# A table written in one contiguous transfer, and the products of a deformable convolution on GpSimd between its gathers

## The chip, the cores and the metric

The kernel runs on one core of one Trainium2 chip. The metric is the device time of the program in microseconds. Three timed runs gave 628.83, 629.05 and 629.80 us; the median is 629.05 us.

## The reference

Four layers follow each other on a batch of four images x of shape (4, 128, 32, 32), float32:

- L0: attention with 32 reduced channels, over the 1024 pixels of an image, with a projection and a residual.
- L1: a bottleneck with a deformable convolution, and a residual. This is where the change lies.
- L2: attention with 16 channels for queries and keys and 128 for values, scaled by gamma, and a residual.
- L3: group norm, attention with 128 channels, projection, residual, divided by the root of 2.

The deformable convolution samples each pixel's nine taps at positions that are themselves computed:

```
off  = conv3x3(h, woff) + boff
y, x = off + base of pixel and tap
mask = sigmoid(off[:, 18:])
samp = (img[y0, x0]*wy0*wx0 + img[y0, x0+1]*wy0*wx1
      + img[y0+1, x0]*wy1*wx0 + img[y0+1, x0+1]*wy1*wx1) * mask
out  = einsum('bckhw,ock->bohw', samp, w2) + b2
```

## The kernel before, in words

Each layer works on one image at a time, with 1024 pixels as eight tiles of 128. The engines' instructions are written out by hand, one program for each engine, with semaphores between them. A first loop of four turns does L0 of image a together with the first part of L1 of image b = a - 1. A second loop does L3 of image a, L2 of image b = a + 1 and the last part of L1, the samples, of image c = a + 2. The last turn of the first loop takes the samples of image 0 in; the first turn of the second loop has no L3, and those of image 1; the last two turns have no samples.

The path of the samples, which the change touches:

- `l1_cells` (ScalarE) writes the 32 channels of the image four times into `cells`, shifted by one row or column, so that one column of `cells` holds the 4 corners x 32 channels of one cell. There are 33 x 33 = 1089 cells.
- `l1_table`: TensorE transposes `cells` in nine chunks of up to 128 columns (the last has 65), ScalarE copies them to `tabS`, and SP writes them to a table in DRAM, `cell_table0` or `cell_table1`, one row of 512 bytes for each cell. Before, this takes two DMAs for an image: 1024 rows in pieces of one row each, and the last 65.
- `l1_coordinates` (VectorE) computes the rows to fetch, `rows_all`, and the weights of the corners, `corner_w`, for the whole image.
- GpSimd (POOL) copies the rows to `rows_cur`, waits for the table (`tab_out`), and then, for each of the eight tiles, waits for a free slot (`slot_free`) and issues nine indirect DMAs (L309), one for each tap: 128 pixels x one row of 512 bytes, into `got[:, t, k, :]`. `got` has eight slots, one for each tile.
- `l1_weigh` (VectorE, L1167) waits until a tile's nine gathers are in (`got_sem[t]`), multiplies 128 x 1152 values by the weights of the corners, each of 36 weights for 32 channels, into `weighed`, and frees the slot. `l1_add` (L1180) adds the four corners into `samples`. Both stand at fixed places in VectorE's order, between the maxima, copies and reciprocals of L2 and L3.
- `l1_turn` (TensorE, ScalarE) transposes the samples into `samplesT`; `l1_conv2` and `l1_conv3` are matmuls over them, and `l1_end` gives the input of L2.

Of the kernel before, what the change touches and what calls it, by code (L numbers as in the profile page):

```python
# [20 lines left out]
N = H * W  # L21
P = 128
# [9 lines left out]
CELLS = H + 1  # L32
TABLE = CELLS * CELLS
TCHUNKS = -(-TABLE // P)
TLAST = TABLE - (TCHUNKS - 1) * P
YX = 2 * TAPS
OFFS = 3 * TAPS
TAPS_A_TURN = 3
# [24 lines left out]
def build(nc, x_dram, weights_dram, out_dram):  # L63
# [5 lines left out]
    with ctx:  # L69
# [4 lines left out]
            return ctx.enter_context(nc.semaphore(name))  # L74


        tables = [nc.dram_tensor(f"cell_table{n}", (TABLE, CORNERS * R), fp32).ap() for n in range(2)]


        wts = sb("wts", [P, WIDTH])  # L80
# [30 lines left out]
        cells = sb("cells", [P, CELLS, CELLS])  # L111
        tabS = sb("tabS", [P, BATCH, TCHUNKS, P])
        x3s = y = cells[:, :, :].rearrange("p a b -> p (a b)")[:, 0:N]


        h2_full = x2_sum = sb("h2_full_x2_sum", [P, N])
# [14 lines left out]
        weighed = sb("weighed", [P, TAPS, CORNERS * R])  # L131
# [79 lines left out]
        sp_go, pool_go = sem("sp_go"), sem("pool_go")  # L211
        got_sem = [sem(f"got{t}") for t in range(TILES)]
        slot_free = sem("slot_free")
        sample_ready = sem("sample_ready")
        st_mm = sem("st_mm")
        st_copied = sem("st_copied")
# [40 lines left out]
        @block.sync  # L257
        def _(sp):
            sp.dma_start(wts[:, 0:FIRST], weights_dram[:, 0:FIRST]).then_inc(weights0_in, 16)
            for b in range(1, BATCH):  # L260
                sp.dma_start(xall[:, b, :], x_view[b]).then_inc(x_in[b], 16)
            tab_pair = tabS[:, :, :, :].rearrange("p (a n) k d -> p a n k d", n=2)
            with sp.Fori(0, BATCH // 2) as i:
                for n, table in enumerate(tables):

                    sp.wait_ge(tab_copied, 6 * i + 3 * n + 3)
                    sp.sem_inc(sp_go, 1)

# [12 lines left out]

            for h in range(2):
                at = slice(h * HALF, (h + 1) * HALF)
                sp.wait_ge(y_ready, BATCH + 1 + h)
                sp.dma_start(out_view[BATCH - 1, :, at], y[:, at]).then_inc(y_out, 16)
            sp.wait_ge(y_out, 16 + 16 * (BATCH + 1))
            for n in range(2):
                sp.wait_ge(tab_out[n], 16 * BATCH)


        @block.gpsimd
        def _(pool):
            rows_pair = rows_all[:, :, :].rearrange("p (a n) k -> p a n k", n=2)
            with pool.Fori(0, BATCH // 2) as i:
                for n, table in enumerate(tables):

                    pool.wait_ge(rows_ready, 2 * i + n + 1)
                    nc.gpsimd.tensor_copy(rows_cur[:, n, :],
                                          rows_pair[:, bass.ds(i, 1), n, :].rearrange("p a k -> p (a k)"))\
                        .then_inc(rows_copied, 1)  # L300
                    pool.wait_ge(rows_copied, 2 * i + n + 1)
                    pool.wait_ge(tab_out[n], 32 * i + 32)
# [12 lines left out]
        def _(pe):  # L315
# [137 lines left out]

            def l1_table(i, n, bank):

                flat = cells[:, :, :].rearrange("p a b -> p (a b)")
# [341 lines left out]
        def _(act):  # L798
# [58 lines left out]
            def l1_table(i, n, bank):  # L857
                act.wait_ge(tab_mm, 3 * i + n + 1)
                first, chunks = PIECES[n][0], len(PIECES[n])
                rows = P if first < TCHUNKS - 1 else TLAST  # L860
                to = tabS[0:rows, bass.ds(i, 1), first:first + chunks, :].rearrange("p i k d -> p (i k) d")
                copy(to, bank[0:rows, 0:chunks * P].rearrange("p (k d) -> p k d", d=P)).then_inc(tab_copied, 1)


            def l1_turn(i, t, bank):
# [211 lines left out]
        def _(dve):  # L1077
# [23 lines left out]

            def l0_denominators(i, samples_too):
                if samples_too:
                    l1_samples(0, 0)
                dve.wait_ge(d4_mm, i + 1)
                nc.vector.tensor_copy(d4, (ys if samples_too else xq)[:, :]).then_inc(d4_copied, 1)
                if samples_too:
                    l1_samples(0, 1)
                    l1_samples(0, 2)
                dve.wait_ge(d_mm, i + 1)  # L1110
                nc.vector.reciprocal(inv[:, :], ys[:, 0:TILES]).then_inc(inv0_done, 1)
                if samples_too:
                    l1_samples(0, 3)

            def l0_end(i):

# [43 lines left out]
                last.then_inc(corner_ready, 1)  # L1160


            def l1_weigh(i, t):

                dve.wait_ge(got_sem[t], 16 * TAPS * (i + 1))
                w = corner_w[:, bass.ds(i, 1), t, :].rearrange("p b k -> p (b k)")
                nc.vector.tensor_tensor(weighed[:, :, :].rearrange("p k (c r) -> p (k c) r", r=R),  # L1167
                                        got[:, t, :, :].rearrange("p k (c r) -> p (k c) r", r=R),
                                        w.rearrange("p (k a) -> p k a", a=1).to_broadcast([P, TAPS * CORNERS, R]),
                                        ALU.mult).then_inc(slot_free, 1)  # L1170
                dve.drain()
                if t == TILES - 1:
                    dve.sem_inc(table_free, 1)

            def l1_add(i, t, early=False):

                if t >= 2 or early:

                    dve.wait_ge(st_mm, TILES * i + t - 1)
                nc.vector.tensor_reduce(samples[:, t % 2, :].rearrange("p (k r) -> p k r", r=R),  # L1180
                                        weighed[:, :, :].rearrange("p k (c r) -> p k r c", r=R),
                                        axis=X, op=ALU.add).then_inc(sample_ready, 1)
                dve.drain()

            def l1_samples(i, t, early=False):
                l1_weigh(i, t)
                l1_add(i, t, early)

            def l1_conv2(i):
                dve.wait_ge(h2_high, 2 * i + 2)  # L1190
# [103 lines left out]
            def second_loop_step(a, b, c):  # L1294
# [15 lines left out]
                for t in range(TILES):  # L1310
                    if L3:
                        l3_turn(a, t)
                    if L2 and t == 0:
                        maximum(2, b, 1, xs)
                    if SAMPLES and t >= 3:
                        l1_weigh(c, t - start)
                    if L3:
                        if t + 1 < TILES:
                            l3_max(a, t + 1, (ys if L2 else (ys, xs)[(t + 1) % 2]))
# [9 lines left out]
                        l2_values(b, 0)  # L1329
                        l2_values(b, 1)  # L1330
                if SAMPLES:
                    l1_samples(c, TILES - start)
                if L3 and L2:
                    l3_end(a)
                elif L3:
# [2 lines left out]
                if L2:  # L1338
                    for n in range(2, TILES):
                        l2_values(b, n)  # L1340
                        if SAMPLES and L3:
                            if n == 2:
                                l1_samples(c, 6)
                            if n == 3:
                                l1_weigh(c, 7)
# [14 lines left out]
                    l2_statistics(1)  # L1360


            nc.vector.memset(cells[:, :, :], 0.0)
# [38 lines left out]
            first_loop_step(BATCH - 1, BATCH - 2, None, samples_too=True)  # L1402

            for t in range(4, TILES):
                l1_samples(0, t)
            for t in range(2):
                l1_samples(1, t, early=True)
            l1_conv2(0)
            l1_end(0)
            l1_coordinates(BATCH - 1, xp)  # L1410
# [88 lines left out]
```

## Time and profile before

| | |
|---|---|
| timed, median of 3 | 629.05 us |
| profiled execution, span | 852.6 us |
| POOL busy | 283.4 us, 33% |
| TensorE busy, matmul | 531.5 us, 62% |
| VectorE busy | 353.6 us, 41% |
| ScalarE busy | 277.5 us, 33% |
| mean granted clock | 0.794 |
| moved by DMA | 27.11 MB, mean 32 GB/s |

The profiled execution's own time is known here only by its span. It is 223.6 us longer than the median of the timed runs, so a duration or an order can be taken from the profile, but a sum of its waits can't be set equal to a sum of the timed run's. Busy shares are averages over stages with different limits. A matmul's end is modelled, and spans of POOL are rough.

### The profile page before, as it was taken

Reading aid. Unit: us, or ns where it says so; the run is one execution under the profiler, and the core shown is the slowest. Engines: PE = TensorE matmul, PEld = TensorE weight load, DVE = VectorE, ACT = ScalarE, POOL = GpSimd, SP = SyncE. Lnnn points to the kernel's source line nnn. Section 1 sums busy time; section 2 is a strip of 40 time slices with the busy share of each in tenths; the row PEclk is TensorE's granted clock in tenths of the full one; section 3 lists DMA queues with packets and bytes.
Section 4 is the critical chain, followed back from the end, with each engine's and each line's share of the span. In section 5 each row is a group of like instructions: output and inputs, shape, how many; then the busy total and the mean of one; then the engine's idle time right before and its main releaser. Section 6 shows DMA issues by size and latency. Waiting matters only on the chain.

```text
span 852.6 us, 7735 instructions
## 1 busy us (share of the span) xinstructions
PE 531.5 (62%) x2840; PEld 362.9 (43%) x2840; DVE 353.6 (41%) x462; ACT 277.5 (33%) x402; POOL 283.4 (33%) x296
## 2 busy tenths in 40 slices
PE   5789930117883065026604897271859998999797
PEld 2445410113542033014502665151636785678576
DVE  4244420002671193129400586151347984752243
ACT  1436510005550041104100554130235633554353
POOL 0000477750037477734775006565520000000000
PEclk8697975558996578556756899585889999999899
DMA  4000111110001121100211001111100000000000
GB/s 166 0 1 1 52 52 53 52 40 26 1 22 53 37 63 52 52 26 22 76 52 43 1 2 40 43 41 43 59 22 0 0 25 0 1 1 16 10 1 25
DMA packets 15298, 27.11 MB, mean 32 GB/s; under 512 B 4900, under 2 KB 9256, under 8 KB 15144
## 3 DMA queue, kind: packets, MB, share of 16 engines
q0 software_dynamic: 9216, 18.89, 7.8%
q1 hardware_dynamic: 5768, 6.20, 2.2%
q10 hardware_dynamic: 288, 1.67, 0.5%
q8 instruction: 17, 0.28, 0.1%
q14 instruction: 9, 0.07, 0.0%
HBM read 22.41 MB, written 4.33 MB: 31 GB/s over the span
## 4 chain that ended last, share of the span: by engine, by line
PE 41%; another core or an unknown queue 30%; DVE 11%; issue 8%; ACT 7%; DVEq 2%; DMA 1%; ACTq 0%
PE ys L559 6%; PE yy L581 5%; PE xq L346 5%; DVE samples L1180 3%; PE yy L572 3%; DVE neg_max L1086 2%; ACT expT L805 2%; PE ys L479 2%; PE xq L319 2%; PE yy L319 2%; PE ys L319 2%; PE xs L325 2%; DVE weighed L1167 2%; PE xq L389 1%
## 5 line engine op out<-in xcount | busy, mean ns | idle before, releaser
L309 POOL DMA_INDIRECT got<-cell_table,rows_cur x288 | 282.2, 980 | 247.5 <-DVE weighed L1167 149.3
L346 PE MATMUL xq<-vT,expT 128*128 128x129 f32 x512 | 68.8, 294 | 14.9 <-ACT oT L898 7.3
L581 PE MATMUL yy<-v3T,probsT 128*128 128x128 f32 x512 | 65.1, 282 | 16.2 <-issue 15.3
L346 PEld LDWEIGHTS xq<-vT,expT 128*128 128x128 f32 x512 | 66.8, 210 | 19.5 <-issue 9.5
L581 PEld LDWEIGHTS yy<-v3T,probsT 128*128 128x128 f32 x512 | 61.7, 196 | 24.5 <-issue 20.2
L1180 DVE TENSOR_REDUCE samples<-weighed 128x288 f32<-128x1152 f32 x32 | 68.9, 2153 | 2.2 <-issue 0.7
L559 PE MATMUL ys<-k,q_offs 128*128 128x512 f32 x112 | 55.1, 616 | 1.3 <-ACT k L924 1.3
L1264 DVE TENSOR_REDUCE neg_max<-ys 128x1 f32<-128x1024 f32 x28 | 34.2, 1222 | 38.6 <-PE ys L559 35.7
L1210 DVE RECIPROCAL inv<-xq 128x1 f32<-128x1 f32 x32 | 5.3, 167 | 103.2 <-remote 68.6
L479 PE MATMUL ys<-samplesT,wts 96*128 96x512 f32 x48 | 29.8, 772 | 27.7 <-issue 27.1
L470 PE MATMUL yy<-wts,samples 128*96 128x128 f32 x72 | 14.1, 313 | 52.2 <-ACT samplesT L800 43.5
L1086 DVE TENSOR_REDUCE neg_max<-xs 128x1 f32<-128x1024 f32 x32 | 38.9, 1217 | 15.1 <-remote 8.6
L1269 DVE COPY probsT<-yy 128x512 f32<-128x512 f32 x32 | 22.0, 689 | 53.9 <-PE yy L572 46.6
L1167 DVE TENSOR_TENSOR weighed<-got,corner_w 128x1152 f32<-128x1152 f32 x32 | 43.5, 1359 | 1.3 <-issue 0.5
L898 ACT ACTIVATE oT<-xq,inv 128x128 f32<-128x128 f32 x28 | 10.3, 367 | 94.9 <-DVE inv L1210 65.2
L572 PE MATMUL yy<-wts,probs 128*128 128x128 f32 x224 | 35.1, 280 | 6.8 <-ACT probs L930 4.8
L800 ACT ACTIVATE samplesT<-yy 96x384 f32<-96x384 f32 x24 | 11.7, 485 | 72.0 <-remote 45.3
L470 PEld LDWEIGHTS yy<-wts,samples 128*96 128x96 f32 x72 | 8.8, 142 | 61.4 <-issue 56.1
L805 ACT ACTIVATE expT<-xs 128x1024 f32<-128x1024 f32 x32 | 32.7, 1020 | 6.2 <-remote 4.3
L572 PEld LDWEIGHTS yy<-wts,probs 128*128 128x128 f32 x224 | 26.3, 143 | 19.1 <-issue 7.6
L930 ACT ACTIVATE probs<-ys,neg_max 128x1024 f32<-128x1024 f32 x28 | 31.2, 1114 | 6.2 <-DVE neg_max L1264 6.1
L340 PE MATMUL ys<-q_stack,k_stack 128*128 128x512 f32 x32 | 14.1, 528 | 30.4 <-issue 19.3
(186 smaller groups left out, 875.4 us busy)
## 6 DMA issues: line engine op xcount, KB each, us to landing
got<-cell_table,rows_cur POOLq DMA_INDIRECT x288
cell_table<-tabS SPq DMA_DIRECT2D x4, 512.0 KB
xall<-x_dram SPq DMA_DIRECT2D x3, 512.0 KB, 9.3
out_dram<-cells SPq DMA_DIRECT2D x3, 512.0 KB, 2.7
wts<-weights_dram ACTq DMA_DIRECT2D x1, 1120.5 KB, 8.9
xall<-x_dram ACTq DMA_DIRECT2D x1, 512.0 KB, 5.0
out_dram<-cells SPq DMA_DIRECT2D x2, 256.0 KB, 2.0
wts<-weights_dram SPq DMA_DIRECT2D x1, 289.0 KB, 4.8
```

Source lines behind the costliest of these rows:

```text
L309: nc.gpsimd.indirect_dma_start(got[:, t, k, :], None, table, bass.IndirectOffsetOnAxis(ap=rows_cur[:, n, at:at + 1], axis=0)).then_inc(got ...
L319: last = nc.tensor.matmul(bank, w, x[:, at], start=True, stop=True)
L346: last = nc.tensor.matmul(to, expT[:, j, t * P:(t + 1) * P], vT[:, j, C - width:C + 1], start=j == 0, stop=j == TILES - 1)
L479: last = nc.tensor.matmul(bank, wt("w2", TR)[:, g * P:(g + 1) * P], samplesT[:, g, at], start=g == 0, stop=g == TURNS - 1)
L559: last = nc.tensor.matmul(to, q3[:, t * P:(t + 1) * P], k3[:, at], start=True, stop=True)
L572: last = nc.tensor.transpose(bank[:, j * P:(j + 1) * P], probs[:, t % 2, at:at + P], ident)
L581: last = nc.tensor.matmul(yo[:, 0:C], probsT[:, j * P:(j + 1) * P], v3T[:, j, :], start=j == 0, stop=j == TILES - 1)
L805: nc.scalar.activation(expT[:, j, :], bank[:, :], ACT.Exp).then_inc(exp_done[L], 1)
L1086: nc.vector.tensor_reduce(neg_max[:, t:t + 1], bank[:, :], axis=X, op=ALU.max, negate=True).then_inc(max_done[L], 1)
L1167: nc.vector.tensor_tensor(weighed[:, :, :].rearrange("p k (c r) -> p (k c) r", r=R), got[:, t, :, :].rearrange("p k (c r) -> p (k c) r", r=R),
L1180: nc.vector.tensor_reduce(samples[:, t % 2, :].rearrange("p (k r) -> p k r", r=R), weighed[:, :, :].rearrange("p k (c r) -> p k r c", r=R) ...
L1264: nc.vector.tensor_reduce(neg_max3[:, t:t + 1], pair[:, :], axis=X, op=ALU.max, negate=True).then_inc(max3_done, 1)
```

## The change

The table in DRAM is padded to 1152 rows. TensorE transposes every ninth column of `cells` (chunk k has the columns 9p + k), so that partition p of `tabS` holds nine rows that lie next to each other in the table, and one DMA for each image writes them, 4608 bytes for each partition. The rows that the gathers fetch are the same.

The multiplication by the corners' weights moves from VectorE to POOL, in place in `got`. POOL issues the gathers of tile t, then multiplies tile t - 1; the last tile's product comes after all gathers of its image. VectorE keeps the addition, which now reads `got`, waits for POOL's `weighed`, and frees the slot afterwards. In VectorE's order the additions stand where products and additions stood, in part later by one step.

```diff
-        tables = [nc.dram_tensor(f"cell_table{n}", (TABLE, CORNERS * R), fp32).ap() for n in range(2)]
+        tables = [nc.dram_tensor(f"cell_table{n}", (PADDED, CORNERS * R), fp32).ap() for n in range(2)]
...
+        cells_padded = sb("cells", [P, PADDED])
+        cells = cells_padded[:, 0:TABLE].rearrange("p (a b) -> p a b", b=CELLS)
...
-                    sp.dma_start(table[0:(TCHUNKS - 1) * P, :].rearrange("(k p) d -> p k d", p=P),
-                                 tab_pair[:, bass.ds(i, 1), n, 0:TCHUNKS - 1, :].rearrange("p a k d -> p (a k) d"))\
-                        .then_inc(tab_out[n], 16)
-                    sp.dma_start(table[(TCHUNKS - 1) * P:TABLE, :],
-                                 tab_pair[0:TLAST, bass.ds(i, 1), n, TCHUNKS - 1, :].rearrange("p a d -> p (a d)"))\
+                    sp.dma_start(table.rearrange("(p k) d -> p (k d)", k=TCHUNKS),
+                                 tab_pair[:, bass.ds(i, 1), n, :, :].rearrange("p a k d -> p (a k d)"))\
                         .then_inc(tab_out[n], 16)
...
+            def weigh(i, n, t):
+                pool.wait_ge(got_sem[t], 16 * TAPS * (2 * i + n + 1))
+                pool.sem_inc(pool_go, 1)
+                parts = got[:, t, :, :].rearrange("p k (c r) -> p (k c) r", r=R)
+                nc.gpsimd.tensor_tensor(parts, parts,
+                                        weight_pair[:, bass.ds(i, 1), n, t, :].rearrange("p a (k b) -> p (a k) b", b=1)
+                                        .to_broadcast([P, TAPS * CORNERS, R]), ALU.mult).then_inc(weighed, 1)
...
                         for k in range(TAPS):
                             at = t * TAPS + k
                             nc.gpsimd.indirect_dma_start(
                                 got[:, t, k, :], None, table,
                                 bass.IndirectOffsetOnAxis(ap=rows_cur[:, n, at:at + 1], axis=0)).then_inc(got_sem[t], 16)
+                        if t == 1:
+                            pool.wait_ge(corner_ready, 2 * i + n + 1)
+                            pool.sem_inc(pool_go, 1)
+                        if t:
+                            weigh(i, n, t - 1)
+                    weigh(i, n, TILES - 1)
...
-                    rows = P if k < TCHUNKS - 1 else TLAST
-                    last = nc.tensor.transpose(bank[0:rows, k % 4 * P:(k % 4 + 1) * P],
-                                               flat[:, k * P:k * P + rows], ident)
+                    last = nc.tensor.transpose(bank[:, k % 4 * P:(k % 4 + 1) * P], strided[:, k, :], ident)
...
-            def l1_weigh(i, t):
-                dve.wait_ge(got_sem[t], 16 * TAPS * (i + 1))
-                w = corner_w[:, bass.ds(i, 1), t, :].rearrange("p b k -> p (b k)")
-                nc.vector.tensor_tensor(weighed[:, :, :].rearrange("p k (c r) -> p (k c) r", r=R),
-                                        got[:, t, :, :].rearrange("p k (c r) -> p (k c) r", r=R),
-                                        w.rearrange("p (k a) -> p k a", a=1).to_broadcast([P, TAPS * CORNERS, R]),
-                                        ALU.mult).then_inc(slot_free, 1)
-                dve.drain()
+            def l1_add(i, t, early=False):
+                dve.wait_ge(weighed, TILES * i + t + 1)
+                if t >= 2 or early:
+                    dve.wait_ge(st_mm, TILES * i + t - 1)
+                nc.vector.tensor_reduce(samples[:, t % 2, :].rearrange("p (k r) -> p k r", r=R),
+                                        got[:, t, :, :].rearrange("p k (c r) -> p k r c", r=R),
+                                        axis=X, op=ALU.add).then_inc(sample_ready, 1)
+                dve.drain()
+                dve.sem_inc(slot_free, 1)
                 if t == TILES - 1:
                     dve.sem_inc(table_free, 1)
```

## Rows read from the trace of the kernel before

**Rows 1.** The page: span, busy time, and POOL's busy tenths in 40 slices.
```profile
span 852.6 us, 7735 instructions
...
PE 531.5 (62%) x2840; PEld 362.9 (43%) x2840; DVE 353.6 (41%) x462; ACT 277.5 (33%) x402; POOL 283.4 (33%) x296
...
POOL 0000477750037477734775006565520000000000
```

**Rows 2.** The page: the chain that ended last, by engine.
```profile
PE 41%; another core or an unknown queue 30%; DVE 11%; issue 8%; ACT 7%; DVEq 2%; DMA 1%; ACTq 0%
```

**Rows 3.** Timelines of TensorE and VectorE: start us, us, engine, line, operation.
```profile
112.70 0.73 PE L325 MATMUL ys<-k_stack,q_stack 96*128 96x512 f32 x2 [0.29 <-issue]
...
140.88 1.22 DVE L1086 TENSOR_REDUCE neg_max<-ys 128x1 f32<-128x1024 f32 x1 [18.39 <-remote]
```

**Rows 4.** Stretches: length, busy us of PE, PEld, DVE, ACT, POOL; clock, DMA share, GB/s.
```profile
94.00:185.00 91.00, 21.77 (x106) 13.59 (x106) 14.99 (x15) 12.29 (x16) 69.08 (x72) 0.63 0.18 51
...
626.00:718.00 92.00, 83.54 (x483) 60.87 (x484) 67.52 (x81) 45.03 (x71) 0.00 (x0) 0.94 0.02 7
```

**Rows 5.** Timeline of POOL: gathers of the first image; duration ns min/median/max of all.
```profile
94.18 1.11 POOL L309 DMA_INDIRECT got<-cell_table,rows_cur  x1 [11.91 <-DMA cell_table<-tabS]
95.59 0.94 POOL L309 DMA_INDIRECT got<-cell_table,rows_cur  x1 [0.30 <-issue]
...
183.96 0.94 POOL L309 DMA_INDIRECT got<-cell_table,rows_cur  x1 [0.30 <-issue]
...
L309 POOL DMA_INDIRECT got<-cell_table,rows_cur x288: 938/944/2128, 94.2 to 624.8; - x144
```

**Rows 6.** The page: groups of gathers, reductions and products, busy us and mean ns.
```profile
L309 POOL DMA_INDIRECT got<-cell_table,rows_cur x288 | 282.2, 980 | 247.5 <-DVE weighed L1167 149.3
...
L1180 DVE TENSOR_REDUCE samples<-weighed 128x288 f32<-128x1152 f32 x32 | 68.9, 2153 | 2.2 <-issue 0.7
...
L1167 DVE TENSOR_TENSOR weighed<-got,corner_w 128x1152 f32<-128x1152 f32 x32 | 43.5, 1359 | 1.3 <-issue 0.5
```

**Rows 7.** Timeline of VectorE and POOL: a product and a gather.
```profile
305.67 1.36 DVE L1167 TENSOR_TENSOR weighed<-got,corner_w 128x1152 f32<-128x1152 f32 x1
305.75 2.10 POOL L309 DMA_INDIRECT got<-cell_table,rows_cur  x1 [0.31 <-issue]
```

**Rows 8.** Timeline of SP, and the page's DMA issues.
```profile
88.52 0.50 SPq L274 DMA_DIRECT2D cell_table<-tabS  x1
...
out_dram<-cells SPq DMA_DIRECT2D x3, 512.0 KB, 2.7
...
out_dram<-cells SPq DMA_DIRECT2D x2, 256.0 KB, 2.0
```

**Rows 9.** Timeline of VectorE: the end of two turns, and the last product.
```profile
629.20 0.74 DVE L1222 SCALAR_TENSOR_TENSOR x<-xs,wts,xall 128x512 f32<-128x512 f32 x1
...
703.44 1.36 DVE L1167 TENSOR_TENSOR weighed<-got,corner_w 128x1152 f32<-128x1152 f32 x1
...
718.62 0.74 DVE L1222 SCALAR_TENSOR_TENSOR x<-xs,wts,xall 128x512 f32<-128x512 f32 x1
```

**Rows 10.** Waits: engine, line, waited for, us in total, times, longest.
```profile
POOL got L309 <- DVE weighed L1167: 149.3, 6, 51.1
```

**Rows 11.** Groups of POOL by shape: copy and smallest fill.
```profile
L298 POOL COPY rows_cur<-rows_all 128x72 int32 x4 | 1.0, 246 | 94.6 <-DVE rows_all L1141 94.6
...
L1491 POOL MEMSET const-float32-0.0<- 128x1 f32 x1 | 0.1, 98 | 0.3 <-issue 0.3
```

**Rows 12.** Timeline of VectorE: low parts of three turns, first product.
```profile
57.96 1.22 DVE L1081 SCALAR_TENSOR_TENSOR k_stack<-yy,k_stack 32x1024 fp32r<-32x1024 f32 x1 [0.49 <-ACT k_stack L800]
...
102.34 1.22 DVE L1081 SCALAR_TENSOR_TENSOR k_stack<-yy,k_stack 32x1024 fp32r<-32x1024 f32 x1 [0.49 <-ACT k_stack L800]
...
219.94 1.22 DVE L1081 SCALAR_TENSOR_TENSOR k_stack<-yy,k_stack 32x1024 fp32r<-32x1024 f32 x1 [0.49 <-ACT k_stack L800]
...
243.15 1.35 DVE L1167 TENSOR_TENSOR weighed<-got,corner_w 128x1152 f32<-128x1152 f32 x1
```

More of the change, by code:

```diff
@@ L34 @@
 TCHUNKS = -(-TABLE // P)
-TLAST = TABLE - (TCHUNKS - 1) * P
+PADDED = TCHUNKS * P
 YX = 2 * TAPS
@@ L110, in build @@
         bn_t = sb("bn_t", [P, 3])
-        cells = sb("cells", [P, CELLS, CELLS])
+        cells_padded = sb("cells", [P, PADDED])
+        cells = cells_padded[:, 0:TABLE].rearrange("p (a b) -> p a b", b=CELLS)
         tabS = sb("tabS", [P, BATCH, TCHUNKS, P])
-        x3s = y = cells[:, :, :].rearrange("p a b -> p (a b)")[:, 0:N]
+        x3s = y = cells_padded[:, 0:N]
         h2_full = x2_sum = sb("h2_full_x2_sum", [P, N])
@@ L130, in build @@
         got = sb("got", [P, TILES, TAPS, CORNERS * R])
-        weighed = sb("weighed", [P, TAPS, CORNERS * R])
         samples = sb("samples", [P, 2, TAPS * R])
@@ L213, in build @@
         slot_free = sem("slot_free")
+        weighed = sem("weighed")
         sample_ready = sem("sample_ready")
@@ L287, in _ @@
             for n in range(2):
-                sp.wait_ge(tab_out[n], 16 * BATCH)
+                sp.wait_ge(tab_out[n], 16 * (BATCH // 2))
         @block.gpsimd
@@ L293, in _ @@
             rows_pair = rows_all[:, :, :].rearrange("p (a n) k -> p a n k", n=2)
+            weight_pair = corner_w[:, :, :, :].rearrange("p (a n) t k -> p a n t k", n=2)
+            def weigh(i, n, t):
[5 more added lines that the diff above has]
+                                        .to_broadcast([P, TAPS * CORNERS, R]), ALU.mult).then_inc(weighed, 1)
             with pool.Fori(0, BATCH // 2) as i:
@@ L301, in _ @@
                     pool.wait_ge(rows_copied, 2 * i + n + 1)
-                    pool.wait_ge(tab_out[n], 32 * i + 32)
+                    pool.wait_ge(tab_out[n], 16 * i + 16)
                     for t in range(TILES):
@@ L454, in l1_table @@
             def l1_table(i, n, bank):
-                flat = cells[:, :, :].rearrange("p a b -> p (a b)")
+                strided = cells_padded[:, :].rearrange("p (a k) -> p k a", k=TCHUNKS)
                 for k in PIECES[n]:
-                    rows = P if k < TCHUNKS - 1 else TLAST
-                    last = nc.tensor.transpose(bank[0:rows, k % 4 * P:(k % 4 + 1) * P],
-                                               flat[:, k * P:k * P + rows], ident)
+                    last = nc.tensor.transpose(bank[:, k % 4 * P:(k % 4 + 1) * P], strided[:, k, :], ident)
                 last.then_inc(tab_mm, 1)
@@ L859, in l1_table @@
                 first, chunks = PIECES[n][0], len(PIECES[n])
-                rows = P if first < TCHUNKS - 1 else TLAST
-                to = tabS[0:rows, bass.ds(i, 1), first:first + chunks, :].rearrange("p i k d -> p (i k) d")
-                copy(to, bank[0:rows, 0:chunks * P].rearrange("p (k d) -> p k d", d=P)).then_inc(tab_copied, 1)
+                to = tabS[:, bass.ds(i, 1), first:first + chunks, :].rearrange("p i k d -> p (i k) d")
+                copy(to, bank[:, 0:chunks * P].rearrange("p (k d) -> p k d", d=P)).then_inc(tab_copied, 1)
             def l1_turn(i, t, bank):
@@ L1103, in l0_denominators @@
                 if samples_too:
-                    l1_samples(0, 0)
+                    l1_add(0, 0)
                 dve.wait_ge(d4_mm, i + 1)
@@ L1107, in l0_denominators @@
                 if samples_too:
-                    l1_samples(0, 1)
-                    l1_samples(0, 2)
+                    l1_add(0, 1)
+                    l1_add(0, 2)
                 dve.wait_ge(d_mm, i + 1)
@@ L1112, in l0_denominators @@
                 if samples_too:
-                    l1_samples(0, 3)
+                    l1_add(0, 3)
             def l0_end(i):
@@ L1180, in l1_add @@
                 nc.vector.tensor_reduce(samples[:, t % 2, :].rearrange("p (k r) -> p k r", r=R),
-                                        weighed[:, :, :].rearrange("p k (c r) -> p k r c", r=R),
+                                        got[:, t, :, :].rearrange("p k (c r) -> p k r c", r=R),
                                         axis=X, op=ALU.add).then_inc(sample_ready, 1)
                 dve.drain()
-            def l1_samples(i, t, early=False):
-                l1_weigh(i, t)
-                l1_add(i, t, early)
+                dve.sem_inc(slot_free, 1)
+                if t == TILES - 1:
+                    dve.sem_inc(table_free, 1)
             def l1_conv2(i):
@@ L1314, in second_loop_step @@
                         maximum(2, b, 1, xs)
-                    if SAMPLES and t >= 3:
-                        l1_weigh(c, t - start)
                     if L3:
@@ L1331, in second_loop_step @@
                 if SAMPLES:
-                    l1_samples(c, TILES - start)
+                    l1_add(c, TILES - start)
                 if L3 and L2:
@@ L1342, in second_loop_step @@
                             if n == 2:
-                                l1_samples(c, 6)
-                            if n == 3:
-                                l1_weigh(c, 7)
+                                l1_add(c, 6)
                             if n == 4:
@@ L1360, in second_loop_step @@
                     l2_statistics(1)
-            nc.vector.memset(cells[:, :, :], 0.0)
+            nc.vector.memset(cells_padded[:, :], 0.0)
             nc.vector.memset(shift[:, :, :], 0.0)
@@ L1404, in _ @@
             for t in range(4, TILES):
-                l1_samples(0, t)
+                l1_add(0, t)
             for t in range(2):
-                l1_samples(1, t, early=True)
+                l1_add(1, t, early=True)
             l1_conv2(0)
```

2 lines of the change are left out of this document (removed).

## The prediction

> **What bounds the kernel now.** The profiled execution spans 852.6 us, while the three timed runs have a median of 629.05 us: 223.6 us apart, so the first task is to find out which parts of the profile the timed runs don't have. The busy shares come first [rows 1]: no engine is full, and GpSimd (POOL) works in blocks that end near three quarters of the span. The chain that ended last [rows 2] gives 30% of the span, about 256 us, to "another core or an unknown queue", though the program has one core. Two rows show what this is [rows 3]: VectorE waits 18.39 us and reads only at 140.88 scores whose matmuls TensorE shows at 112.70. The stretches [rows 4] say when it happens. From 94 to 185 us POOL issues all 72 gathers of one image, and TensorE is busy for 21.8 of 91 us at a granted clock of 0.63. After 626 us no gather is left, TensorE is busy for 83.5 of 92 us, and the granted clock is 0.94. So the unexplained waits go with the gathers, and their sum is near what the timed runs lack. I take them for a cost of the recorded execution, and rebuild the timed one from two lines that these waits don't touch. That is a choice; the trace doesn't prove it.
>
> **The gather line.** Nine gathers fetch one tile, eight tiles make an image, and there are four images: 288 gathers. The first starts at 94.18 us, the 72nd at 183.96, and the median instruction is 0.944 us with 0.30 us between two [rows 5], 1.248 from start to start (of the 71 steps from the first gather to the last, 89.78 us, or 1.265 each with the lengthened ones). An image takes 72 x 1.248 = 89.9 us. The sum of all 288 [rows 6] is 282.2 us, 10.3 more than 288 x 0.944 = 271.9. Gathers that are lengthened explain that excess: one took 2.10 us beside a product that VectorE ran from 305.67 us [rows 7]. Landing after issue isn't shown for a gather; the nearest rows are output transfers, 2.0 us for 256 KB [rows 8]. Back to back, the last tile is there at 94.2 + 4 x 89.9 + 10.3 + 2.0 = 466.1 us. In the profile, the last product starts at 703.44 us and the span ends 149.2 us later, all of it without gathers [rows 9]. Together: 615.3 us.
>
> **The engine line.** In the same undisturbed part the start of one turn of the second loop can be read from VectorE's last additions of the turn before, 629.20 and 718.62 us [rows 9]: 89.4 us a turn, against 89.9 for an image's gathers. The two are level, so gathers that grow longer can't hide. The waits of POOL for VectorE, 149.3 us in six places [rows 10], don't speak against this: they are the engines' delays of the recorded execution, handed on through buffers that come free late.
>
> Against the median, 629.05 - 615.3 = 13.8 us remain: what lies around the span, and what my line leaves out. I carry them unchanged.
>
> **The change, part by part.**
>
> *Table in one DMA.* Before, the second of the first table's two DMAs is issued at 88.52 us, and the gather that waits for both starts at 94.18 [rows 5, 8]: 5.7 us. Output of the same 512 KB with long rows lands in 2.7 us [rows 8]; with 4.6 KB runs I expect about that, so the gathers start 3 us earlier, at 91.2. The bounds are no gain and 5.7 us. Later tables are written while POOL still gathers the image before, and that cover is kept, as POOL becomes later. The strided transposes and the last chunk's 128 rows instead of 65 cost TensorE and ScalarE at most some tenths of a microsecond for each table, beside the image's attention; without that cover, only the first table's would count.
>
> *The product moves to POOL.* VectorE loses 32 products of 1.36 us, 43.5 us in all [rows 6]. Its reduction (2.15 us) keeps its size. POOL gains 32 products, and queues behind each are the next tile's nine gathers; SP's queue is not passed. Price of one: the trace has no such operation on POOL. The lower bound is VectorE's 1.36 us for the same shape. For POOL itself, a fill of one element takes 0.10 us and a copy of 72 elements 0.246 [rows 11]: 0.1 us fixed and 2.0 ns an element, so 1152 elements cost 0.1 + 2.3 = 2.4 us with one source. A product reads two sources; at twice that it is 4.7 us, the upper bound. I take 2.4, since the second source here is only one value for every 32 elements, and with the issue gap of 0.3 it is 2.7 us.
>
> The Trainium skill (GPSIMD Engine Reference, Elementwise — side-by-side cycle accounting) gives 4497 ns as measured for a tensor_tensor add of 2048 elements on GpSimd, 1.96 times VectorE's; scaled to 1152 that is an estimate of 2.53 us, which would add 4 us to my sum. Its table of engine selection advises against elementwise work there.
>
> *New waits.* Product t-1 comes after gathers t, so 11.2 us cover the landing. The eighth product has no gathers in front of it and waits for its tile: 2.0 us an image, and behind it stand the next image's gathers. An image on POOL then costs 89.9 + 8 x 2.7 + 2.0 = 113.5 us. The wait for the weights of the corners at tile 1 costs nothing: VectorE writes them before the first gather's tile is in.
>
> *Slots.* A slot comes free after VectorE's reduction, some 2.2 us later than now. Turns of the first loop are 44.4 us apart (57.96 to 102.34), the last starts its low part at about 146.7, and its first product comes 23.2 us later [rows 12], at 170. The second image's gathers start at 91.2 + 113.5 = 204.7, so the slot is long free. In later turns the same: VectorE reduces each tile as it comes.
>
> *The gathers get back* at most the 10.3 us by which they were lengthened, already left out of the 113.5. In the Trainium skill (SBUF — State Buffer, SBUF: two separate sides) VectorE with two SBUF inputs and GpSimd exclude each other on a shared port pair; the 2.10 us gather agrees. By that rule the change gives these microseconds back, and its reductions, which have one input, wouldn't block the new products.
>
> **Sum.** 91.2 + 4 x 113.5 = 545.2 us for the last product. From the end of the last product to the end of the span were 852.6 - 704.8 = 147.8 us [rows 9]. 545.2 + 147.8 + 13.8 = 706.8; I say 707 us, 12% slower. The engine line doesn't reach this: a turn needs 89.4 us less up to 8 x 1.36, against 113.5. With 1.36 us a product the sum is 91.2 + 4 x (89.9 + 8 x 1.66 + 2.0) + 147.8 + 13.8 = 674; with 4.7, 91.2 + 4 x (89.9 + 8 x 5.0 + 2.0) + 161.6 = 780.
>
> **Rivals.**
>
> *Gathers are faster in a timed run, and POOL has room (other side: faster).* The 0.30 us between gathers may belong to the recording. At 0.944 us, the new line is 91.2 + 4 x (68.0 + 21.6 + 2.0) = 457.6 us for the last product; today's time puts the need for it at 629.05 - 149.2 - 13.8 = 466. So the line isn't felt, and VectorE's relief of 8 x 1.36 = 10.9 us in the last turn may show: about 618 us. It decides below 0.97 us a gather, where 72 gathers take 70 us. For it: gathers leave 0.30 us with no stated reason. Against it: at 1.248 the old line explains the median with 14 us to spare, which faster gathers would leave as 30 or more. Chance 8%, and 3% that the two sides cancel to no change.
>
> *Gathers between the two.* At 1.1 us, 91.2 + 4 x (79.2 + 23.6) + 161.6 = 664 us. Chance 9%.
>
> *The product is as cheap as on VectorE:* 674 us, chance 12%. For it, the plain access pattern; against it, the copy's 2.0 ns an element.
>
> *The product costs both reads, or waits for VectorE:* 740 to 780 us, chance 13%. For it: two sources, and the gathers show that the two engines can hold each other up. Against it: the small operand.
>
> *The table transfer is not shortened:* 3 us more on the forecast; not a case of its own.
>
> **Numbers.** My forecast, a product of 2.1 to 3.2 us with gathers at 1.25, has 55% and its own range of 690 to 730 us. The range of 655 to 765 leaves out the fast gathers and the dearest products. Faster than today by over 0.2% (about what a measurement of this kernel can tell from no change): 0.08. Within it: 0.03. Slower: 0.89.
>
> **What would show it.** The page after should have POOL with 32 products of 2.4 us at spacing 2.7 from the next gather, and VectorE without its 43.5 us. A POOL block of one image should last about 113 us where nothing else holds it, with a short wait for a landing before each eighth product. The first gather should start 3 us earlier relative to the table's issue, and no gather should be lengthened beside a reduction. VectorE should wait for POOL's products in the second loop. The profiled span itself may move otherwise than the timed one, as the unexplained waits go with the gathers. My forecast is wrong if timed gathers run closer than 1.25 us, or if the product is far from 2.4 us.

## The result, and the profile after

The changed kernel takes 676.1 us (median of 4, 674.11 to 676.79), the kernel before 628.94 us (median of 4, three of them the runs already given). The measured ratio is 1.0771, with a 95% interval of 1.0743 to 1.0799: 7.7% slower; the two medians alone divide to 1.075, inside that interval. Medians and ratios below leave out an execution that took over 1.5% more than the fastest of its kernel. The forecast was 707 us, in a range of 655 to 765; the narrower range of its main case, 690 to 730, is missed.

From the page after: span, busy time, POOL's busy tenths, the chain that ended last, and the groups of gathers, reductions and products.

```profile
span 675.0 us, 7787 instructions
...
PE 518.8 (77%) x2840; PEld 357.0 (53%) x2840; DVE 315.3 (47%) x430; ACT 276.4 (41%) x402; POOL 345.5 (51%) x328
...
POOL 0000037787877788777877878788878100000000
...
POOL 47%; PE 24%; issue 17%; DVE 4%; ACT 4%; DMA 2%; DVEq 1%; POOLq 1%; ACTq 0%; SPq 0%
...
L317 POOL DMA_INDIRECT got<-cell_table,rows_cur x288 | 276.2, 959 | 97.1 <-issue 82.5
L1180 DVE TENSOR_REDUCE samples<-got 128x288 f32<-128x1152 f32 x32 | 68.8, 2151 | 109.8 <-POOL got L299 109.2
L299 POOL TENSOR_TENSOR got<-got,corner_w 128x1152 f32<-128x1152 f32 x32 | 68.3, 2140 | 0.6
```

The span is 675.0 us and this execution's own time 676.79, so hardly 2 us lie around a span. The chain has no unknown queue any more: 47% of it is POOL. Against [rows 1], POOL's block is now filled from the first gather on. The product has left VectorE, and POOL has 32 of them at 2.14 us.

POOL's timeline for the first image: start us, duration us, engine, line, operation, what it waited for.

```profile
93.78 1.15 POOL L317 DMA_INDIRECT got<-cell_table,rows_cur  x1 [11.36 <-DMA cell_table<-tabS]
...
115.51 0.94 POOL L317 DMA_INDIRECT got<-cell_table,rows_cur  x1 [0.30 <-issue]
116.55 2.15 POOL L299 TENSOR_TENSOR got<-got,corner_w 128x1152 f32<-128x1152 f32 x1
118.86 0.99 POOL L317 DMA_INDIRECT got<-cell_table,rows_cur  x1 [0.16 <-issue]
...
196.32 0.94 POOL L317 DMA_INDIRECT got<-cell_table,rows_cur  x1 [0.30 <-issue]
197.28 4.22 POOL L299 TENSOR_TENSOR got<-got,corner_w 128x1152 f32<-128x1152 f32 x2
...
202.53 1.01 POOL L317 DMA_INDIRECT got<-cell_table,rows_cur  x1 [0.86 <-POOL rows_cur L306]
```

A product begins within 0.1 us of the end of the ninth gather, and a gather follows 0.16 us after it. From the start of a tile's last gather to the start of the next tile's first are 3.35 us here and 3.26 in 22 of the 24 such places, where there were 1.25: a product adds 2.01 us. At the end of the image two products stand together, 4.22 us, and the next image's first gather comes at 202.53, 108.75 us after the first one; the two images behind it take 108.0 us each.

The whole line after: ns min/median/max of each group, its first and last start; the last row is the time from a gather's issue to its landing. The single row below is SP's issue of the first table.

```profile
L317 POOL DMA_INDIRECT got<-cell_table,rows_cur x288: 940/944/1789, 93.8 to 520.0; - x144
L299 POOL TENSOR_TENSOR got<-got,corner_w x32: 2126/2141/2150, 116.5 to 523.0; 128x1152 f32<-128x1152 f32 x32
...
DMA to landing us min/median/max: 2.3/2.5/3.6
```

```profile
88.18 0.33 SPq L272 DMA_DIRECT2D cell_table<-tabS  x1
```

The last gather starts at 520.0 us and the two last products end at 525.15; 149.85 us later the span ends. The tail is that of [rows 9], 147.8 us, plus 2. The first gather starts 5.60 us after the table's issue, against 5.7 in [rows 5, 8].

### The profile page after: what moved, and what is told of

Its sections match the earlier page's. It is cut to its first block, busy times and chain, and to the rows that moved or that the text cites. A ratio compares the mean times of both kernels' runs of the same rounds, so it can differ in the third digit from the quotient of the medians.

```text
span 675.0 us, 7787 instructions
## 1 busy us (share of the span) xinstructions
PE 518.8 (77%) x2840; PEld 357.0 (53%) x2840; DVE 315.3 (47%) x430; ACT 276.4 (41%) x402; POOL 345.5 (51%) x328
## 4 chain that ended last, share of the span: by engine, by line
POOL 47%; PE 24%; issue 17%; DVE 4%; ACT 4%; DMA 2%; DVEq 1%; POOLq 1%; ACTq 0%; SPq 0%
POOL got L317 39%; POOL got L299 7%; PE yy L593 4%; PE ys L571 3%; PE xq L360 2%; PE yy L584 2%; ACT expT L817 1%; PE xs L339 1%; PE ys L491 1%; PE xq L333 1%; DVE neg_max L1097 1%; PE yy L333 1%; PE xs L571 1%; PE xq L372 1%; PE ys L333 1%
## 5 line engine op out<-in xcount | busy, mean ns | idle before, releaser
L317 POOL DMA_INDIRECT got<-cell_table,rows_cur x288 | 276.2, 959 | 97.1 <-issue 82.5
L1180 DVE TENSOR_REDUCE samples<-got 128x288 f32<-128x1152 f32 x32 | 68.8, 2151 | 109.8 <-POOL got L299 109.2
L299 POOL TENSOR_TENSOR got<-got,corner_w 128x1152 f32<-128x1152 f32 x32 | 68.3, 2140 | 0.6
L593 PEld LDWEIGHTS yy<-v3T,probsT 128*128 128x128 f32 x512 | 60.1, 192 | 8.4 <-ACT probsT L812 4.3
L593 PE MATMUL yy<-v3T,probsT 128*128 128x128 f32 x512 | 63.2, 277 | 0.9 <-ACT probsT L812 0.9
L571 PE MATMUL ys<-k,q_offs 128*128 128x512 f32 x112 | 53.4, 599 | 1.3 <-ACT k L935 1.3
L482 PE MATMUL yy<-wts,samples 128*96 128x128 f32 x72 | 15.3, 333 | 48.9 <-DVE samples L1180 29.7
L339 PE MATMUL xs<-k_stack,q_stack 96*128 96x512 f32 x64 | 26.5, 501 | 9.4 <-DVE neg_max L1097 4.7
```

What stands on the lines that cost most here:

```text
L299: nc.gpsimd.tensor_tensor(parts, parts, weight_pair[:, bass.ds(i, 1), n, t, :].rearrange("p a (k b) -> p (a k) b", b=1) .to_broadcast([P, ...
L317: nc.gpsimd.indirect_dma_start(got[:, t, k, :], None, table, bass.IndirectOffsetOnAxis(ap=rows_cur[:, n, at:at + 1], axis=0)).then_inc(got ...
L339: last = nc.tensor.matmul(to, q_stack[0:3 * R, t * P:(t + 1) * P], k_stack[0:3 * R, at], start=True, stop=True)
L571: last = nc.tensor.matmul(to, q3[:, t * P:(t + 1) * P], k3[:, at], start=True, stop=True)
L593: last = nc.tensor.matmul(yo[:, 0:C], probsT[:, j * P:(j + 1) * P], v3T[:, j, :], start=j == 0, stop=j == TILES - 1)
```

## The experiments

**e9: the kernel before, recorded once more.** No edit. It comes first because everything else is measured against it.

> The kernel before, unchanged, profiled once more. Theory (the waits of 8 to 50 us beside the gathers were an accident of that one recorded execution): a span of 622 to 630 us, POOL's gathers back to back from 94 to about 471 us, and no share of the chain for an unknown queue. Rival (this kernel's two DMAs for the table together with products on VectorE bring them on whenever it is recorded): a span above 750 us.

Measured: 627.35 us and a span of 625.3, in a single run; nine timed runs of the same kernel beside it lie at 625.25 to 627.69. From its page: span, chain, gathers and products.

```profile
span 625.3 us, 7735 instructions
...
POOL 46%; PE 27%; issue 16%; DVE 4%; ACT 4%; DMA 2%; DVEq 1%; POOLq 0%; SPq 0%; ACTq 0%
...
L309 POOL DMA_INDIRECT got<-cell_table,rows_cur x288 | 289.7, 1006 | 100.7 <-issue 86.5
...
L1167 DVE TENSOR_TENSOR weighed<-got,corner_w 128x1152 f32<-128x1152 f32 x32 | 43.5, 1360 | 37.5 <-DMA got<-cell_table,rows_cur 36.9
```

The stretch from 94 to 185 us (length, then busy us of PE, PEld, DVE, ACT and POOL, clock, DMA), and the whole line as above:

```profile
94.00:185.00 91.00, 81.81 (x454) 46.96 (x454) 54.55 (x73) 48.19 (x62) 69.36 (x72) 0.91 0.21 58
```

```profile
L309 POOL DMA_INDIRECT got<-cell_table,rows_cur x288: 940/944/2117, 93.9 to 472.7; - x144
L1167 DVE TENSOR_TENSOR weighed<-got,corner_w x32: 1332/1358/1403, 169.4 to 475.3; 128x1152 f32<-128x1152 f32 x32
```

In the same stretch TensorE is busy for 81.8 us instead of the 21.8 of [rows 4], beside the same 72 gathers. So the waits of [rows 3] were an accident of one recorded execution, and belong neither to the kernel nor to gathers. What the first profile hid is seen here: POOL gathers back to back from 93.9 to 472.7 us, and makes 46% of the chain. The excess of the gathers over 288 x 0.944 us is 17.8 us instead of 10.3, because more gathers meet products: 20 of the lengthened ones here, 12 in the first recording.

**e1: the contiguous table alone.** The kernel before with this edit (and the padded names, transposes and copies that go with it):

```diff
-                    sp.dma_start(table[0:(TCHUNKS - 1) * P, :]...)
-                    sp.dma_start(table[(TCHUNKS - 1) * P:TABLE, :]...)
+                    sp.dma_start(table.rearrange("(p k) d -> p (k d)", k=TCHUNKS), ...)
```

> The kernel before with the contiguous table alone; the products stay on VectorE. Theory (the product on GpSimd makes all of the loss): within 3 us of the time before, 626 to 629 us, since the first table lands only about 0.4 us earlier and later tables are covered. Rival (strided transposes or the wider transfer cost something that the loss contains): above 632 us. If the profile of this kernel again spans far more than its timed runs, the unexplained waits belong to gathers beside products on VectorE or to chance; if it agrees with the timed runs, it also shows the undisturbed order that the kernel before has.

Measured: 629.48 us against 629.31, ratio 1.000 (0.9976 to 1.0023); span 623.7. Within the 0.24% of this interval, 1.5 us, the table is worth nothing and costs nothing.

**e5: the products alone.** The changed kernel with the old table, the reverse of the edit of e1.

> The changed kernel with the old table in two DMAs; the products are on GpSimd. Theory (all of the loss is the products', the table is worth nothing): 674 to 679 us. Rival (the contiguous table hid part of the loss, as it lands a little earlier and in fewer packets): above 681 us.

Measured: 676.72 us, ratio 1.0777 (1.0741 to 1.0813). With e1 this puts all of the loss on the products.

**e2: no product on VectorE.** The kernel before; 1120 of 1152 values of each product are left out, and the reduction reads a buffer of zeros.

```diff
-                nc.vector.tensor_tensor(weighed[:, :, :]..., got[:, t, :, :]..., w..., ALU.mult).then_inc(slot_free, 1)
+                nc.vector.tensor_tensor(weighed[:, 0, 0:R], got[:, t, 0, 0:R],
+                                        w[:, 0:1].to_broadcast([P, R]), ALU.mult).then_inc(slot_free, 1)
```

> The kernel before with VectorE's product cut from 1152 to 32 values a partition (the other products are left out; the reduction reads a constant buffer). Theory (GpSimd's gather line sets the time, products only lengthen gathers): 10 us less at most, 617 to 627 us. Rival (VectorE is in the path, as it loses 43 us of work): 585 to 612 us.

Measured: 610.7 us, ratio 0.9716 (0.9688 to 0.9745), 18.6 us less. The time lies outside the theory's numbers and inside the rival's, so the expectation missed, and the time alone would speak for the rival. The trace says which mechanism it was. The group of gathers, busy us and mean ns:

```profile
L309 POOL DMA_INDIRECT got<-cell_table,rows_cur x288 | 274.4, 953 | 100.6 <-issue 86.5 <-DMA cell_table<-tabS 11.4 <-POOL rows_cur L298 1.8
```

The gathers' sum is 15.3 us below that of e9 (274.4 against 289.7), and the last product is 1.2 us shorter: together the 16.6 us between the spans (625.3 and 608.7). VectorE's 43 us were not in the path by themselves, apart from the last product. What they cost was paid by POOL.

**e3: no product on GpSimd.** The changed kernel, with 1120 of 1152 values of each product left out.

```diff
-                nc.gpsimd.tensor_tensor(parts, parts, weight_pair[:, bass.ds(i, 1), n, t, :]...
+                nc.gpsimd.tensor_tensor(parts[:, 0:1, :], parts[:, 0:1, :], weight_pair[:, bass.ds(i, 1), n, t, 0:1]...
```

> The changed kernel with GpSimd's product cut from 1152 to 32 values a partition (the others are left out). Theory (each product stands in full in the gather line, 2.06 us a tile, and nothing else was lost): 32 x 1.9 = 61 us less than the changed kernel, but with the wait for the last tile's landing of each image now open: about 620 us, 615 to 628. Rival (waits added by the new order, such as slots or corner weights, cost some of it): above 635 us.

Measured: 622.09 us, ratio to the kernel before 0.9885 (0.9839 to 0.9931), 54 us below the changed kernel, and inside the 615 to 628 expected. The bulk of 1120 values is worth 54 / 32 = 1.7 us a product: the instruction is 1.89 us shorter (0.25 against 2.14), less the landings that come into the open. The remaining 11 us over e2 are small instructions of 0.25 us with their gaps, and a wait of 1.5 us for the landing in each image, which in the changed kernel the product in front covers. The new order adds no large wait.

**e4: eight gathers a tile.** Contiguous table, products on VectorE; the ninth tap is left out and reads zeros.

```diff
-                        for k in range(TAPS):
+                        for k in range(TAPS - 1):
```

> The kernel with the contiguous table and products on VectorE, with eight gathers a tile instead of nine (the ninth tap is left out and reads zeros). Theory A (the gather line alone sets the time, engines have room): 32 x 1.25 = 40 us less, about 588 us. Theory B (gather line and engine line are level, 89.9 against 89.4 us a turn): only part of it, 605 to 622 us. Rival (engines alone set the time): 626 us or more.

Measured: 596.0 us, ratio 0.9494 (0.9452 to 0.9536), 33 us less of the 40 removed. That is between the two theories, 588 us and 605 to 622, and in the range of neither.

```profile
L307 POOL DMA_INDIRECT got<-cell_table,rows_cur x256: 941/947/2130, 94.7 to 433.7; - x128
L1162 DVE TENSOR_TENSOR weighed<-got,corner_w x32: 1305/1357/1420, 165.2 to 445.7; 128x1152 f32<-128x1152 f32 x32
```

The last gather starts at 433.7 us and could be used some 3.5 us later, but its product runs only at 445.7. So with eight taps the engines' line takes over, and by the last tile the engines are some 8 us behind the gathers; TensorE has 48% of the chain on its page and POOL 21%. This fits most of the 7 us that the removed gathers did not give back. In e9 the last product still waited 4.86 us for its gather.

**e6: half of the products on GpSimd,** those of the odd tiles.

```diff
+                        if t and t % 2 == 0:
+                            weigh(i, n, t - 1)
+                    weigh(i, n, TILES - 1)
...
             def l1_weigh(i, t):
+                if t % 2:
+                    return
```

> Contiguous table, products of the odd tiles on GpSimd between its gathers, of the even tiles on VectorE. Theory (the gather line is the path over its whole length, so each product costs its 2.06 us and gives back the lengthening of the gathers beside it): halfway, 629 + 0.5 x 47 = 653 us, 647 to 658. Rival (the loss needs all products, since some slack covers the first ones): below 643 us. Rival (the loss is the new waits of the order, not the products): above 662 us.

Measured: 656.18 us (median of three, 653.28 to 661.28; a fourth execution took 663.46), ratio 1.0429 (1.0384 to 1.0473), inside the 647 to 658 expected. The profiled execution is the one of 661.28. Busy us, mean ns, and idle time before, with what ended it:

```profile
L318 POOL DMA_INDIRECT got<-cell_table,rows_cur x288 | 286.6, 995 | 98.8 <-issue 83.0 <-DMA cell_table<-tabS 11.4 <-POOL rows_cur L307 2.7
L300 POOL TENSOR_TENSOR got<-got,corner_w 128x1152 f32<-128x1152 f32 x16 | 34.2, 2135 | 7.6 <-DMA got<-cell_table,rows_cur 7.2
```

16 products add 16 x 2.03 = 32 us. Nothing of them is covered. But the gathers' excess stays at 14.7 us, as the other sixteen products on VectorE still meet them, and 7.2 us of landings come into the open, since the last tile's product has no product in front of it. So half the products cost somewhat more than half the loss: 4.3% of 7.7, though the interval reaches down to 3.84, which is the half.

**e7: the table earlier.** With the line known, its start can be moved. Contiguous table, products on VectorE, and:

```diff
                     l1_offsets_turn(b, 2, xp)
+                    l1_offsets_turn(b, 3, xp)
+                    pe.wait_ge(v_ready[0], a + 1)
+                    for piece, bank in enumerate((xo, yt, yo)):
+                        l1_table(b, piece, bank)
                 for j in range(TILES):
                     l0_shifted(a, j)
-                    ... (turn 3 at j == 1, the table at j == 4, 5, 6)
```

and ScalarE's copies likewise ahead of the exponentials.

> Contiguous table, products on VectorE, and the table transposed and copied ahead of the shifted scores of the first loop instead of among them. Theory (the time is the first gather's start plus four images of gathers plus a fixed tail): the first gather starts at 86 to 88 us instead of 94, the engines come 1 to 2 us a turn later, and the time falls by 4 to 8 us, to 621 to 625 us. Rival (the engines' line is level with the gathers', and each turn grows by the work put in front): no change or slower, 628 to 634 us.

Measured: 620.63 us, ratio 0.9880 (0.9854 to 0.9905), at the edge of the 621 to 625 expected.

```profile
L307 POOL DMA_INDIRECT got<-cell_table,rows_cur x288: 940/944/2126, 87.5 to 468.2; - x144
...
L307 POOL DMA_INDIRECT got<-cell_table,rows_cur x288 | 291.7, 1013 | 92.5 <-issue 86.5 <-DMA cell_table<-tabS 3.3 <-POOL rows_cur L296 2.7
```

The first gather starts at 87.5 us instead of 94.0. Of these 6.5 us, 4.7 are the earlier issue of the table (83.80 against 88.46 in e1) and 1.8 a shorter landing, 2.76 us against 4.54; why the first table lands late in its old place stays open. Of the 6.5 us the last gather keeps 2.9 (468.2 against 471.1), because more gathers now meet products: their excess is 19.8 us, against 16.1 in e1.

**e10: the product in three pieces.** Contiguous table in its old place, and:

```diff
+                for a, b in [(0, 12), (12, 24), (24, 36)]:
+                    last = nc.vector.tensor_tensor(weighed...[:, a:b, :], got...[:, a:b, :], w[:, a:b]..., ALU.mult)
+                last.then_inc(slot_free, 1)
```

> Contiguous table, table in its old place, VectorE's product in three pieces. Theory (gathers are held up until the piece beside them ends): gathers' busy time falls from 288.2 us to about 280, the time to 616 to 621 us. Rival (the two changes only pay together, as the engines had to be moved as well): 625 us or more.

Measured: 616.89 us, ratio 0.9841 (0.9813 to 0.9870), as expected, though VectorE works 0.3 us more for each tile.

```profile
L307 POOL DMA_INDIRECT got<-cell_table,rows_cur x288 | 280.9, 975 | 100.6 <-issue 86.2 <-DMA cell_table<-tabS 11.3 <-POOL rows_cur L296 2.7
```

Why shorter pieces help is seen in the trace of e9: one product and the two gathers that it meets.

```profile
204.20 0.95 POOL L309 DMA_INDIRECT got<-cell_table,rows_cur  x1 [0.30 <-issue]
...
204.41 1.36 DVE L1167 TENSOR_TENSOR weighed<-got,corner_w 128x1152 f32<-128x1152 f32 x1 [1.55 <-DMA got<-cell_table,rows_cur]
...
205.46 1.13 POOL L309 DMA_INDIRECT got<-cell_table,rows_cur  x1 [0.30 <-issue]
```

The gather that had started before the product keeps its length. The one that starts while the product runs ends 0.82 us after the product's end, and so does the lengthened gather of [rows 7]. In e9, 33 gathers start while a product runs, and 31 of them end 0.82 us after it; 24 gathers have a product start beside them, and their median stays at 0.944 us. So a gather is held until the instruction that was running at its start ends, and a shorter piece holds it for less.

**e8 and e11: early table with three and with six pieces.**

> As the one before, and VectorE's product in three pieces of 384 values instead of one of 1152, so that a gather that meets it waits for a shorter piece. Theory (gathers are held up until a two-input instruction of VectorE ends): the gathers' sum of busy time falls by some 8 us of the 16 us of excess, and the time by 4 to 8 us more, to 614 to 620 us. Rival (the hold-up is per instruction, or three pieces hit three gathers): no gain over the one before, or a loss of up to 5 us.

> Early table and six pieces of 192 values. Theory: the hold-up halves again, some 4 us less of gathers, while VectorE spends 0.45 us more a tile, 14 us in all; the gather line goes to its floor and the engines take over: 604 to 609 us, hardly under three pieces. Rival (VectorE's added work is in the path): 611 us or more.

Measured: 608.4 us with three pieces, ratio 0.9678 (0.9649 to 0.9706), and 606.88 us with six, ratio 0.9688 (0.9669 to 0.9707), each against the kernel before beside it; the two intervals overlap. e8 comes out lower than the 614 to 620 expected, e11 inside its 604 to 609. In e8 the first gather starts at 84.9 us, 2.6 before that of e7 with the same order up to there; what brings this is not shown. First e8, then e11 with its chain:

```profile
L307 POOL DMA_INDIRECT got<-cell_table,rows_cur x288: 940/944/1969, 84.9 to 455.2; - x144
L1158 DVE TENSOR_TENSOR weighed<-got,corner_w x96: 508/552/630, 171.8 to 458.7; 128x384 f32<-128x384 f32 x96
...
L307 POOL DMA_INDIRECT got<-cell_table,rows_cur x288 | 281.2, 977 | 92.5 <-issue 86.2 <-DMA cell_table<-tabS 3.3 <-POOL rows_cur L296 2.7
```

```profile
PE 40%; POOL 23%; DVE 15%; issue 11%; ACT 5%; DVEq 4%; DMA 2%; POOLq 0%; SPq 0%; ACTq 0%
...
L307 POOL DMA_INDIRECT got<-cell_table,rows_cur x288 | 278.8, 968 | 92.5 <-issue 86.5 <-DMA cell_table<-tabS 3.3 <-POOL rows_cur L296 2.7
```

The excess over 271.9 us is 9.3 us with three pieces and 6.9 with six. With six, TensorE and VectorE hold more of the chain than POOL: the line of the gathers has lost the lead, and nothing finer than six pieces was tried. Both versions beat the kernel before and the changed one.

## Why the prediction was right in kind and off by 31 us

*What bounds the kernel: right.* The gather line sets the time before and after (POOL 46% and 47% of the chain in e9 and after), and e4 shows both that fewer gathers pay and that the engines are close behind. *The choice to leave out the unexplained waits: right, with a wrong reason.* They went with the recording (e9), not with recorded gathers: in the changed kernel and ten further ones, gathers are recorded without them.

*The forecast summed to 706.8 us; the changed kernel measured 676.1.* The result lies in the wide range, but outside the 690 to 730 of the main case, although both conditions of that case hold: a product of 2.1 to 3.2 us and gathers at 1.25. Four terms were off:

- *The product's step on POOL, 2.7 us, was 2.03 on average.* The copy's slope of 2.0 ns an element gave 2.4; the instruction took 2.14, and the issue gap of 0.30 us that I added is hardly there: 0.16 us stand behind a product and none to 0.1 in front of it, in place of the 0.30 between two gathers. 32 x 0.67 = 21 us too much. The page of the Trainium skill (GPSIMD Engine Reference, Elementwise — side-by-side cycle accounting) led to an estimate of 2.53 us; the measurement is 15% below it.
- *The landing of each image's last tile, 2.0 us, costs nothing.* I took the eighth product to wait. But the seventh product stands between the last gather and it, so that a gather's 2.5 us of landing, counted from its issue, are covered. 8 us too much.
- *What lies around the span, 13.8 us, is 2.* The rest was missing from my line of the kernel before: it put the last tile at 466.1 us, where e9 starts the last product at 475.3. The first profile, in which POOL stood idle for long, shows too little lengthening (10.3 us against 17.8), and 0.8 to 0.9 us at each of three image ends were left out. 12 us too much.
- *The earlier first gather, 3 us, was not there.* The first table lands 4.64 us after its issue, not 2.7, and the start moves by 0.1 us relative to the issue. The 2.7 was right for the transfer by itself: issued earlier, in e7, e8 and e11, it lands in 2.76 us. 2.6 us too little.

These make 21 + 8 + 12 - 2.6 = 38 us. Against them stand 9 us that the sum had left out: 2.5 us of copies and gaps between images, 4.4 us of excess in the gathers that remain, and 2 us of the tail. That leaves 30 us too much against the profiled execution, and 31 against the median. All the large terms erred on the dear side, and the wide range took that in.

*Where the loss goes,* from e9 to after, first gather to last: 378.8 us become 426.2. Thirty products lie between, and with their gaps they add 60.9 us, 2.03 each; the gathers' busy time falls by 13.5 us (289.7 to 276.2), although a gather behind a product takes 0.99 us instead of 0.944. 60.9 - 13.5 = 47.4. The rest of the 49.7 us between the spans is 1.2 us at the last product and 1.2 us in the tail, less 0.1 at the start.

*The gathers get time back: right, and mis-sized* (10.3 us stated as the most, 13.5 measured). The Trainium skill (SBUF — State Buffer, SBUF: two separate sides) says that VectorE's instructions with two SBUF inputs and those of GpSimd that read SBUF exclude each other, and that on VectorE those with at most one don't, outside the modes in which such an instruction takes both ports. e2, e8, e10 and e11 agree, and so does the changed kernel: 41 of its gathers meet nothing on VectorE but sample reductions, and their median is 0.944 us. Its remaining excess of 4.4 us is mostly beside other two-input instructions of VectorE and behind the products.

*The engines' relief is worth nothing: right.* VectorE now waits for POOL's products:

```profile
DVE samples L1180 <- POOL got L299: 109.2, 12, 23.0
```

```profile
226.94 2.10 DVE L1180 TENSOR_REDUCE samples<-got 128x288 f32<-128x1152 f32 x1 [23.04 <-POOL got L299]
```

The row of 23.04 us is the first tile of the second image. *The slots: right;* the two gathers around an image's end stand 6.2 us apart, and POOL waits for no reduction. *Rivals.* The fast gathers fell: 1.248 us is the timed distance too, since spans of 675.0 us and times of 676.79 agree. The product as cheap as on VectorE was the nearest in time, 674 us, yet not in mechanism; its closeness comes from the other terms' errors.

## What to carry to other kernels

Find the queue that runs back to back and price a moved instruction on it in full, however idle its engine looks: here POOL is half idle over the span, and the 30 products between its gathers cost 61 us, while all 32 free 43 us of an engine that had room. Look, too, for what the moved work did to that queue from where it was, since splitting VectorE's product where it stood gained 1.6% (e10) and moving it lost 7.8% (e5). And where a profile's span is far from the timed runs, record it once more before a sum is built on it.

## What the runs showed of the hardware

- A product of 128 x 1152 float32 values with a broadcast second source takes GpSimd 2.14 us and VectorE 1.36, a ratio of 1.57.
- A gather of 128 rows of 512 bytes costs POOL 0.944 us and a gap of 0.30, and lands 2.5 us after its issue. The gap is there before another gather; before a product it is 0.1 us or less, and behind one 0.16.
- The excess of 288 gathers follows the length of VectorE's two-input pieces: 16 to 20 us at 1.36 us a piece, 9 at 0.55, 7 at 0.35, 2.5 to 4.6 where VectorE has none or a stub of 32 values.
- A gather that starts while VectorE runs a two-input product ends 0.82 us after it (31 of 33 in e9); a product that starts after the gather doesn't lengthen it.
- It holds the other way round too: in the changed kernel, two small two-input instructions of VectorE, 0.23 and 0.22 us elsewhere, took 2.37 and 1.85 us beside a product on POOL and ended 0.10 and 0.03 us after it; in e5 the same two took 2.38 and 1.82 us.
- One recorded execution held waits of up to 53 us for nothing that the profile shows ("remote"), which none of the twelve other recordings has. What brought them on stays open.
